# A decoder of two interleaved streams: both streams' tables of turns placed anew, TensorE's idle products left out

## Time and profile before

| | |
|---|---|
| median of 3 runs | 4543.98 us (4533.97 to 4562.33) |
| span of the profiled execution | 4543.7 us; no time outside it is reported |
| PE, DVE, ACT, POOL busy | 85%, 68%, 44%, 14% of the span |
| mean granted TensorE clock | 0.868 |
| up to the end of the first stretch | 215.2 us |
| the seven rounds | 542.6 to 546.8 us each, 3816.3 us together |
| last stretch | 430.2 us |
| final experts | 82.0 us |

### The profile page before, as it was taken

One profiled execution on the slowest core, in us unless ns is written; L12 is line 12 of the kernel. 1 busy time (PEld: TensorE's weight loads), 2 busy tenths in 40 slices (PEclk: granted clock), 3 DMA queues, 4 the chain that ended last, 5 costly groups with the idle time before them and its releaser, 6 DMA issues. The chain is left out here.

```text
span 4543.7 us, 93495 instructions
## 1 busy us (share of the span) xinstructions
PE 3844.6 (85%) x37090; PEld 2702.1 (59%) x37090; DVE 3103.1 (68%) x8220; ACT 2006.0 (44%) x4862; POOL 650.2 (14%) x988
## 2 busy tenths in 40 slices
PE   3788898888878888788898889888898888889886
PEld 3565565656656665565665656655565655666664
DVE  4467767576775768667686776767767676775782
ACT  2244463443535345363443535345463443535441
POOL 2010201101020110101101011110201101021003
PEclk7788988898988989788897988989988887988997
DMA  6000000000000000000000000000000000000002
GB/s 156 1 2 1 9 1 9 2 1 9 1 9 1 8 2 1 9 1 8 2 7 3 1 8 2 9 2 1 9 1 9 2 1 9 1 8 2 1 1 96
DMA packets 52803, 45.61 MB, mean 10 GB/s; under 512 B 8354, under 2 KB 48914, under 8 KB 52126
## 3 DMA queue, kind: packets, MB, share of 16 engines
q1 hardware_dynamic: 48076, 33.04, 2.7%
q0 software_dynamic: 2560, 5.79, 0.3%
q10 hardware_dynamic: 1714, 0.54, 0.1%
HBM read 27.25 MB, written 12.62 MB: 9 GB/s over the span
## 5 line engine op out<-in xcount | busy, mean ns | idle before, releaser
L763 PE MATMUL banks<-scratch 32*128 32x512 f32 x2048 | 497.0, 708 | 28.6 <-DVE scratch L909 10.8
L331 ACT ACT_TABLE_LOAD x299 | 383.6, 1283 | 7.5 <-PE banks L1090 2.2
L873 ACT ACTIVATE scratch<-banks 128x512 f32<-128x512 f32 x512 | 277.2, 599 | 199.9 <-PE banks L797 199.0
L909 DVE TENSOR_REDUCE scratch<-banks 128x4 f32<-128x512 f32 x512 | 321.8, 680 | 39.1 <-PE banks L736 16.5
L1601 PE MATMUL banks<-scratch,w_ident 128*128 128x256 f32 x1024 | 289.1, 407 | 53.4 <-DVE scratch L1752 52.6
L1885 PE MATMUL banks<-scratch 32*32 32x32 f32 x10496 | 270.4, 217 | 68.2 <-issue 52.8
L1746 DVE TENSOR_TENSOR_SCAN scratch<-scratch 128x512 f32<-128x512 f32 x256 | 312.8, 1222 | 11.5 <-ACT scratch L1689 6.2
L1885 PEld LDWEIGHTS banks<-scratch 32*32 32x32 f32 x10496 | 236.6, 130 | 117.3 <-issue 73.9
L1689 ACT ACTIVATE scratch<-scratch,ssm_A 128x256 f32<-128x256 f32 x512 | 228.6, 505 | 112.0 <-DVE scratch L1746 102.9
L763 PEld LDWEIGHTS banks<-scratch 32*128 32x128 f32 x2048 | 167.8, 203 | 185.1 <-DVE scratch L909 56.3
L1227 PE MATMUL banks<-experts,scratch 128*128 128x128 f32 x1792 | 243.6, 281 | 9.4 <-ACT scratch L1263 8.4
(11 more groups left out here) (522 smaller groups left out, 8414.1 us busy)
## 6 DMA issues: line engine op xcount, KB each, us to landing
expert_in<-scratch SPq DMA_DIRECT2D x1, 4112.0 KB, 28.8
experts<-in_e_W SPq DMA_DIRECT2D x14, 256.0 KB, 5.5
scratch<-expert_in SPq DMA_DIRECT2D x2, 1542.0 KB, 10.8
w_e_W<-in_e_W SPq DMA_DIRECT2D x3, 704.0 KB
experts<-in_e_w SPq DMA_DIRECT2D x1, 1792.0 KB, 9.8
experts<-in_e_w SPq DMA_DIRECT2D x2, 896.0 KB, 13.5
scratch<-expert_in SPq DMA_DIRECT2D x2, 514.0 KB, 5.2
0_xres<-in_x SPq DMA_DIRECT2D x8, 128.0 KB, 2.1
```

The source lines that it names most:

```text
L331: act.preload_act_table_set(name)
L763: last = pe.matmul(row_tiles(t), lhs[r, col(s)], rhs[r, s], start=True, stop=letter == "S" and mask is None, skip_group_check=True)
L873: P.give(act.activation(pT[:, s % 2, j, :], t, ACT.Exp), f"{nm}.T{s}{j}")
L909: P.give(dve.tensor_reduce(negm[:, s, NI * j:NI * j + NI], row_tiles(t), X, ALU.max, negate=True), f"{nm}.S{s}{j}")
```

## The change

Every character of `TURNS` and `LAST_TURNS` for PE, ACT, DVE and POOL is set anew, and the "w" are gone. The number of "0" and "1" in each string of the round is what it was (PE 403 and 403, and so on), as it is in the last stretch (PE 403 and 218, ACT 235 and 124, DVE 294 and 147, POOL 39 and 15), so each stream's steps are the same, in the same order within the stream. SP's string of the round stays; in the last stretch one "0" is written out at its end that `in_turns` appended before. Only the interleaving of the two streams differs. The other code is untouched (`in_turns` and `warm` too).

```diff
@@ -63,48 +63,46 @@
 FIRST = [r[0] != "L0_delta" for r in ROUND]
 TURN = [1, 0]
 TURNS = [
-    ("111ww0001000011010111000111100101wwwwww101111110011000100000001100000000011011011111101111010011011100000000"
-     "1110www00011111111010111111111111111111111111111111101001111101101111101111100110110001111110100000110111110"
...
-     "www1111111111www1111111111111111111111111111111111111111111"),
...
+    ("10100100001010010011101011011111011111110011010000001100100100000100111100001111011010101111100010010101011"
+     "11010100010111111111111111111111011100101110111010111111111101101111111110011111110010110101110010100010101"
...
+     "101111110110111110111111111111111111111111111111111111111"),
...
-    ("110010000000001110000001110000000110111101101111001111011100011111110000101110"),
+    ("010101000000100111000000110000001101101111001111010111011101101011110000111100"),
     ("111000"),
 ]
 LAST_TURNS = [
-    ("111ww00011000001wwwwwwwwwwww01ww000101100011111111111100www10000011100000000000000001100000100100000100wwwww"
...
+    ("10101010000101010001010101011111111010111010110010000101000000000000100100000000001000000011111111111000111"
...
-    ("11001"),
+    ("110010"),
 ]
```

More of the change, by code:

```diff
@@ L75 @@
[L75 to L85, removed]
@@ L86 @@
-    ("110010000000001110000001110000000110111101101111001111011100011111110000101110"),
+    ("10100100001010010011101011011111011111110011010000001100100100000100111100001111011010101111100010010101011"
+     "11010100010111111111111111111111011100101110111010111111111101101111111110011111110010110101110010100010101"
+     "01101110000111110111111001110000111101110110111001111011100111010110001101011011111010011110000101001001010"
+     "11000010100111000000001001110001111001011010000010100001000000000000000000000100000010111100010001010000001"
+     "01011000000100000010011100011101101000000000000010011011111011011010010001000011001100000011011011101000001"
+     "11100110000000000000000000010101000011110000010110000001001010000101110111101001100110110001000110100000100"
+     "10010001100000000100000100101100000000100000001010000011101110101011101011101001101001100010001010111010101"
+     "101111110110111110111111111111111111111111111111111111111"),
@@ new lines @@
+    ("01010101000000001101011110111110000100011001010011100101001001010101010000010100011111011111110101111101111"
+     "01001011111100111110111011111100111110111001101111101110011001011100110000011010001011000011001010000100110"
+     "00010011101010011000000011111001001101100001010000100000111010101010000000111110111000011010001101100010101"
+     "01001100000101111000000001010010000110001001110101100001000000001000110011011001110100010011110100101001100"
+     "101101111101101100000110111101110111111111"),
@@ new lines @@
+    ("01010101000100111011011101001110111010000000001100000010001110001010100111101010011111001110001010101010110"
+     "00001011100100100001111001001110110001010001011101100111111101101101110101111000110011011101101001000101000"
+     "01011011111011110111110100101011001101111000011100011110110001010001000000000010010000111000000010010000011"
+     "00011101111011101100101111001010110000001001010110111000011011110011010001111100110111110010011101111001000"
+     "01100111101111111100000100100000100010101100000000110100000011001000010101100000110110011101100100001000100"
+     "00000111110000111010011001011011101111111111111111111"),
@@ L106 @@
-    ("110001000000001100010000000000011100000000111100001010"),
-    ("11001"),
+    ("10101010000101010001010101011111111010111010110010000101000000000000100100000000001000000011111111111000111"
+     "01100101110010110111110101001101000011100011100010011110001111101101100100110111101110101010110010101000000"
+     "00000000100111011100110100100000101000000000110000000000101000100011100100100000100000000100000011000010000"
+     "00001100111001000100000001000101111011011000100110000000000000000011101101000010101101100100111100000000110"
+     "11010001001000110000010000000010000000000000000001101110000110011101001000010011000001010000000000010000010"
+     "00101010100000100000000001100000011011001001100010000001100110000000001000000000000000"),
@@ new lines @@
+    ("10101000100110000001011110110111000100100101000000000100000000000000011111001101010101000001001111111100100"
+     "01101010001101111111110000101111110001111001110000010000011010110010100010011001101101111101010011000100101"
+     "01000001000001100100100000010000000100000000110000000001001000000000000000000000000001010000000010100000000"
+     "00100000000101010011010100100100000000"),
+    ("01101011111110010001010100100111110000001000000000001101001101000000100011000111011100000111100010000110000"
+     "01000101100100000000010100101001000011010000101000010000000001000000101000101101000100100000101000011001000"
+     "10010000000010000100000000000101111010010100101110000110000000001110000001011011101111011010101010110011010"
+     "00000000111000111100001110110110000000000001001011100100001100000000011000000001001100000000110100010000000"
+     "0001000000000"),
@@ L108 @@
+    ("101010000000010100000110000000010100000000111110000100"),
+    ("110010"),
 ]
```

## The result

The changed kernel takes 4367.2 us (4361.1 to 4369.2, 4 runs) against 4543.7 us: a ratio of 0.9617, with a 95% interval of 0.9588 to 0.9645. The forecast was 4475 us; the gain is 176 us instead of 68.

A forecast was written before the change was run, and what follows sets the result against it. The prediction took PE as the bound for most of a round, the rest being idle time. Its terms, -52 - 32 + 16 + 0 = -68 us, took 4543.7 to 4475 us, own range 4400 to 4498, wide range 4320 to 4590.

The forecast's parts named there:

- part 4: New interleaving of the two streams, judged by PE's waits: taken as 0, bounds 146 us either way.
- Rival A: Placement also covers a quarter of PE's idle time: about 4330 us, chance 0.22.
- Part 1: Idle products on PE removed: they delay ready matmuls by 7.3 us a round, so -52 us.
- Part 3: PE's clock falls by 0.02 without the products, 2 us a stretch: +16 us; bound 11 us a stretch.
- Rival B: Without products PE's clock falls to 0.82 on average in a round: slower, some 4650 us, chance 0.20.
- Part 2: ACT table loads, 39 to 31 a round, 21 to 27 in the last stretch: half counts, -32 us.
- The marks named ahead: Signs of being right: rounds near 536 us, 31 and 27 loads, PE busy some 20 us less, idle about 70.
- the prediction's own test for part 4: Prediction wrong if PE's idle time in a round moves by more than 15 us either way.
- the wide range: Whole-kernel time of 4320 to 4590 us, taking in Rival A's centre and the milder half of Rival B.

The follow-up runs named there:

- e1: The kernel before, in its old order, with the idle products left out and nothing else changed: 4566.7 us, ratio 1.0048 to the kernel before.
- e7: The changed kernel with a different table set loaded ahead of each ACT table load, 249 loads more: 4586.9 us, ratio 1.0093 to the kernel before.
- e13: e1 with only the steps that the new order starts between 165 and 262 us of a round put in the new order: 4485.8 us, ratio 0.9868.
- e14: The changed kernel with only the stretch from 165 to 262 us of each round put back in the old order: 4495.8 us, ratio 0.9897.
- e10: e1 with only the steps that the new order has started by 47 us into a round put in the new order: ratio 0.9951.
- e6: e1 with only the second half of each round put in the new order: 4597.6 us, ratio 1.0109.

## Why the prediction was wrong

- *The step that failed is part 4.* It took the placement at 0, as "the rows favour neither side", with bounds of 146 us. Measured (e1 against the changed kernel), the order gives 196 us, of which 43 are loads by e7's slope: 153 us are left for the placement, over the bound too. I had looked at PE's waits and at the work of the other stream between PE's steps. The largest piece lies where DVE was held back, which was 68% busy and of which I said that it had 30% to spare: one stretch, worth 82 us (e13) to 127 us (e14), in which mamba's scans stood behind waiting instructions of the other stream. That the order on DVE alone would give this is argued from the timelines. The first 47 us of a round give 44 more (e10), for a reason that stays open. Rival A had the right direction and size (4330 us), but by the wrong way: it wanted less idle time on PE, which stayed (73.4 and 75.8 us a round).
- *Part 1 read the delays rightly, but they were not what leaving the products out is worth.* It took 7.3 us a round; the account gives 6.7. But leaving them out cost 22 us in the old order, where parts 1 and 3 together expected to save 36, and the account puts that on the clock.
- *Part 3 was mis-sized.* It took 2 us a stretch; e1's account shows 16.2 a round, above its bound of 11. The slope had been taken between rounds of one program, which all have the same products; it says little about a program without them. Rival B had the mechanism, and in e1 it is there, though milder (a mean clock of 0.851, not 0.82); in the changed kernel the clock rose instead (0.868 to 0.88), as the new order gave back more than the products had held.
- *Part 2 held,* as far as known: 43 us by e7's slope, against 32 taken; two thirds of a load on the path instead of half.
- *The marks named ahead:* 31 and 27 loads, no products, as said; rounds of 520 instead of 536 us; PE's idle time still about 70 (75.9), as said. It moved by less than 15 us, so the prediction's own test for part 4 would have cleared it wrongly: the placement showed in PE's busy time, which fell by 31 us a round instead of 20. The total came near rival A's and inside the wide range although the terms were wrong in both directions (placement +153 us of gain, products -22 instead of +36); the range owed that to A's bound, not to its reason.

## What to carry to other kernels

Where two instruction streams share engines that each run one program in order, look for the instruction that waits while work of the later stream stands behind it, on every engine and not only on the busiest: the timeline shows it as an idle time ahead of one stream's instruction, followed at once by one of the other's that had long been ready. Judge filler work by where it lies: in true waits it raised the clock for little or nothing, and measured waits of a profile were a better guide for it (85 us) than the old positions (10 us, not told from nothing). An account of a busy engine by clock and idle time tells where time shows, not what causes it; exchanging parts of the order told that.

## What was not expected

- Two loads of the same table set in a row leave one record in the trace (249 instead of 498) and no time; whether the second was dropped before it reached the chip is open.
- A table load added on an engine that is busy for 45% costs 0.87 us of its 1.283 (e7).
- The work of PE at full clock, worked out from busy time and clock, comes out at 396 to 405 us a round in the six kernels of the account, whose rounds last 511 to 550 us.
- Why the new second half loses 28 us behind the old first half (e6), and what makes the 44 us of the first 47 us of a round, is open: no run took these apart.
